# A per-token threshold search by bisection: 16 steps instead of 18, and the interval held as lower end and half width

## The reference

```python
xn = _layernorm(x)                          # x: (2, 4096, 4096)

s = silu(einsum('bsh,ih->bsi', xn, w_gate)) # I = 11008 values per token
k = int(0.5 * I)
_, idx = top_k(-abs(s), k)                  # the k smallest in magnitude ...
s[rows, idx] = 0.0                          # ... are set to zero, token by token
s = s * einsum('bsh,ih->bsi', xn, w_up)
attn = einsum('bsi,hi->bsh', s, w_down)

base = einsum('bsd,od->bso', xn, W_base) + b_base
gate = softmax(xn @ W_gate.T)               # 8 experts of rank 16
thr = sigmoid(xn @ W_thr + b_thr) * 0.125
w = max(gate - thr, 0), normalized
moe = einsum('ner,ne,eor->no', xn @ A_w, w, B_w) * 2
out = x + attn + base + moe
```

## Time and profile before

| | us |
|---|---|
| the two timed runs | 5919.37, 6205.86 |
| their median | 6062.61 |
| the profiled execution | 5898.11 |
| its span, slowest core (core 2) | 5896.6 |
| spans of all eight cores | 5871.0 to 5896.6 |
| TensorE busy | 4396.2 (75% of the span) |
| VectorE busy | 1320.0 (22%) |
| ScalarE busy | 1240.5 (21%) |

### The profile page before, as it was taken

How to read it: one execution, slowest core, us unless ns; L and a number is a source line. 1 busy time by engine, 2 the same in 40 slices (tenths; PEclk the granted TensorE clock), 3 DMA queues, 4 the chain that set the end, 5 groups by cost and what they waited for, 6 DMA issues and landing times.

```text
span 5896.6 us, 51357 instructions; the slowest of 8 cores (5871.0 to 5896.6 us)
## 1 busy us (share of the span) xinstructions
PE 4396.2 (75%) x20408; PEld 1983.5 (34%) x20408; DVE 1320.0 (22%) x1928; ACT 1240.5 (21%) x1522; POOL 546.6 (9%) x640
## 2 busy tenths in 40 slices
PE   5999957600399977999859998675004999788988
PEld 2444523200144443433324444232002444333333
DVE  2000052688510000000020000536884001000000
ACT  2000043566400022000020001436663000320000
POOL 0111101000011100111101111010000111001110
PEclk9999978855699977999969999787557999779999
DMA  6999967700399955999959999576004999569999
GB/s 119 146 147 146 126 91 108 112 0 0 49 151 150 151 85 77 171 167 167 165 115 147 145 148 129 82 123 96 0 0 62 150 150 150 72 92 162 168 169 146
DMA packets 669369, 683.02 MB, mean 116 GB/s; under 512 B 31184, under 2 KB 651728, under 8 KB 668112
## 3 DMA queue, kind: packets, MB, share of 16 engines
q0 software_dynamic: 631120, 612.61, 74.0%
q1 hardware_dynamic: 38016, 67.13, 3.7%
HBM read 1267.07 MB, written 25.17 MB: 219 GB/s over the span
## 4 chain that ended last, share of the span: by engine, by line
PE 65%; ACT 12%; DMA 11%; DVE 6%; issue 5%; DVEq 0%; ACTq 0%; SPq 0%; POOLq 0%; POOL 0%
PE q L370 20%; PE q L476 19%; PE q L519 16%; ACT sc L604 10%; PE q L428 8%; DMA wst<-wdT 6%; DMA wst<-wbT 3%; PE pt L492 2%; ACT S L627 1%; DVE st L769 1%; DMA ovr<-x 1%; DVE lns L665 1%; DVE S L828 0%; ACT S L553 0%; ACT sc L627 0%
## 5 line engine op out<-in xcount | busy, mean ns | idle before, releaser
L476 PE MATMUL q<-wst,xT 128*128 128x512 f16 (+1 forms) x5632 | 1203.6, 375 | 870.5 <-DVE S L828 850.6
L370 PE MATMUL q<-wst,xT 128*128 128x512 f16 (+1 forms) x5632 | 1219.3, 375 | 25.3 <-ACT S L553 9.4
L519 PE MATMUL q<-wst,S 128*128 128x512 f16 x4128 | 1145.3, 386 | 17.1 <-DVE ovr L847 16.8
L476 PEld LDWEIGHTS q<-wst,xT 128*128 128x128 f16 x5632 | 549.1, 98 | 1525.4 <-issue 905.6
L604 ACT ACTIVATE sc<-ovr,st 128x6400 f16<-128x6400 f16 x144 | 810.6, 5629 | 254.5 <-DVE st L806 214.9
L370 PEld LDWEIGHTS q<-wst,xT 128*128 128x128 f16 x5632 | 548.2, 98 | 696.1 <-issue 84.9
L781 DVE TENSOR_SCALAR_CACHE_REDUCE sc<-ovr,st 128x4608 f16<-128x4608 f16 x144 | 721.8, 5012 | 65.5 <-ACT sc L604 47.9
L519 PE MATMUL q<-wst,sc 128*128 128x512 f16 x1376 | 531.7, 386 | 85.0 <-DMA wst<-wdT 84.6
L519 PEld LDWEIGHTS q<-wst,S 128*128 128x128 f16 x4128 | 409.5, 99 | 522.9 <-issue 56.9
L428 PE MATMUL q<-wst,xT 128*128 128x512 f16 x2048 | 475.3, 397 | 145.7 <-DMA wst<-wbT 145.7
L842 DVE TENSOR_TENSOR ovr<-q,ffst 128x512 f32<-128x512 f32 x64 | 44.2, 690 | 1526.1 <-PE q L519 1321.4
(11 more groups left out here) (79 smaller groups left out, 1094.1 us busy)
## 6 DMA issues: line engine op xcount, KB each, us to landing
wst<-wgT POOLq DMA_DIRECT2D x168, 1024.0 KB, 9.6
wst<-wuT POOLq DMA_DIRECT2D x168, 1024.0 KB, 11.2
wst<-wdT POOLq DMA_DIRECT2D x160, 1024.0 KB, 11.7
wst<-wbT POOLq DMA_DIRECT2D x64, 1024.0 KB, 11.2
ovr<-x SPq DMA_DIRECT2D x8, 2048.0 KB, 8.7
xs<-x SPq DMA_DIRECT2D x64, 256.0 KB, 10.4
y<-ovr SPq DMA_DIRECT2D x64, 256.0 KB, 7.9
wst<-wdT POOLq DMA_DIRECT2D x16, 768.0 KB, 9.7
```

What stands on the lines that cost most here:

```text
L370: mm = mark(tensor.matmul(quad[m][:, 0:wl], xT[:, k * 512 + m * 128: k * 512 + (m + 1) * 128], wst[:, slot * SLOTB + kk * wl: slot * SLOTB ...
L476: mm = mark(tensor.matmul(bk[:, 0:wl], xT[:, k * 512 + m * 128: k * 512 + (m + 1) * 128], wst[:, slot * SLOTB + kk * wl: slot * SLOTB + (k ...
L519: mm = mark(tensor.matmul(bk[:, 0:512], lhs, wst[:, slot * SLOTB + kk * 512: slot * SLOTB + (kk + 1) * 512], start=(k == 0), stop=(k == IT ...
```

## The change

The number of iterations goes from 18 to 16. The interval is no longer kept by its two ends but by `lo` and `wdh`, half its width; `wdh` takes the column of `hi`. The maximum goes to `mid` first, is halved into `wdh` and copied to `mid`. In each iteration the count is turned into a 0 or 1 in fp32 (`predf`, which is `cu`), one instruction adds `predf * wdh` to `lo`, one halves `wdh`, and one adds `lo` and `wdh` to the new `mid`. After the last iteration VectorE waits for its own last `mid`, doubles `wdh` again and adds it to `lo`, which gives the upper end in the place of `mid`; the masks take that as `hi`. The interval ends four times as wide. ScalarE's program changes in the number of passes alone; TensorE's, GpSimd's and SyncE's don't change.

```diff
--- before.py
+++ after.py
@@ -23,7 +23,7 @@
 NW = len(WINS)
 NWV = O // 512
 SUB = 8
-ITERS = 18
+ITERS = 16
 SEL_L = 4608
 SEL_R = I - SEL_L
 K_TOP = I // 2
@@ -762,18 +762,19 @@
                             di(ins)
                 for m in range(NT):
                     lo = st[:, 3 * m:3 * m + 1]
-                    hi = st[:, 3 * m + 1:3 * m + 2]
+                    wdh = st[:, 3 * m + 1:3 * m + 2]
                     mid = st[:, 3 * m + 2:3 * m + 3]
+                    predf = cu[:, :]
                     vector.wait_ge(aGE, n_aGE(c, NW - 1, m))
                     n = di(vector.memset(lo, 0.0))
-                    n = di(vector.reduce_max(hi, S[:, m * I:(m + 1) * I],
+                    n = di(vector.reduce_max(mid, S[:, m * I:(m + 1) * I],
                                              axis=mybir.AxisListType.X,
                                              apply_absolute_value=True))
                     dw(n)
-                    n = di(vector.tensor_add(mid, lo, hi))
-                    dw(n)
-                    dc(vector.tensor_scalar(out=mid, in0=mid, scalar1=0.5,
-                                             scalar2=None, op0=OP.mult), vMID)
+                    n = di(vector.tensor_scalar(out=wdh, in0=mid, scalar1=0.5,
+                                                scalar2=None, op0=OP.mult))
+                    dw(n)
+                    dc(vector.tensor_copy(mid, wdh), vMID)
                     for it in range(ITERS):
                         vector.wait_ge(vMID, n_vMID(c, m, it))
                         if it == 0:
@@ -788,24 +789,29 @@
                         vector.wait_ge(aCR, n_aCR(c, m, it))
                         dw(n)
                         n = di(vector.scalar_tensor_tensor(
-                            out=cu[:, :], in0=cl[:, 1:2], scalar=0.5,
+                            out=predf, in0=cl[:, 1:2], scalar=0.5,
                             in1=cl[:, 0:1], op0=OP.mult, op1=OP.add))
                         dw(n)
                         n = di(vector.tensor_scalar(
-                            out=pred[:, 0:1], in0=cu[:, :], scalar1=K_EFF,
-                            scalar2=None, op0=OP.is_ge))
-                        n = di(vector.tensor_scalar(
-                            out=pred[:, 1:2], in0=cu[:, :], scalar1=K_EFF,
+                            out=predf, in0=predf, scalar1=K_EFF,
                             scalar2=None, op0=OP.is_lt))
                         dw(n)
-                        n = di(vector.copy_predicated(hi, pred[:, 0:1], mid))
-                        n = di(vector.copy_predicated(lo, pred[:, 1:2], mid))
+                        n = di(vector.scalar_tensor_tensor(
+                            out=lo, in0=predf, scalar=wdh, in1=lo,
+                            op0=OP.mult, op1=OP.add))
+                        n = di(vector.tensor_scalar(
+                            out=wdh, in0=wdh, scalar1=0.5, scalar2=None,
+                            op0=OP.mult))
                         dw(n)
-                        n = di(vector.tensor_add(mid, lo, hi))
-                        dw(n)
-                        dc(vector.tensor_scalar(
-                            out=mid, in0=mid, scalar1=0.5, scalar2=None,
-                            op0=OP.mult), vMID)
+                        dc(vector.tensor_add(mid, lo, wdh), vMID)
+                    vector.wait_ge(vMID, n_vMID(c, m, ITERS))
+                    n = di(vector.tensor_scalar(
+                        out=wdh, in0=wdh, scalar1=2.0, scalar2=None,
+                        op0=OP.mult))
+                    dw(n)
+                    n = di(vector.tensor_add(mid, lo, wdh))
+                    dw(n)
+                    hi = mid
                     n = di(vector.tensor_scalar(
                         out=junkL, in0=sab[:, 0:SEL_L], scalar1=hi,
                         scalar2=None, op0=OP.is_gt))
```

## The result

| | before | after |
|---|---|---|
| profiled execution | 5898.11 us | 5771.03 us |
| its span, slowest core | 5896.6 | 5769.1 |
| median of the cores' spans, cores 0-3 / 4-7 | 5878.8 / 5877.2 | 5740.4 / 5740.6 |
| timed runs, lowest | 5910.79 | 5761.71 |
| timed runs, median of all | 6064.0 (10 runs) | 5961.85 (11 runs) |

The kernel is 2.46% faster. In 7 of the 11 runs of after the cores of one die were granted a lower TensorE clock than the others (in the run of 5990.26 us 0.83 to 0.84 against 0.88) and took 3 to 9% longer, 5 of the 10 runs of before are longer too, by 5 to 9%, and the ratio is that of the other runs, whose medians are 5772.4 and 5918.2 us, 145.8 apart.

The account below looks back on a forecast made before the run. Mostly TensorE and weights bound the span, with the search exposed before the up projection; per chunk 59.5 + 14.8 - 1.1 + 0.4 = 73.6, two chunks 147 us off 5898.1, giving 5751 us; range 5730 to 5785, reported time 5725 to 5910.

Parts of the forecast that it names:

- 286 / 2 = 143 us higher, at 5894: Upper reach of the reported time if it is a median over runs 286 us apart; with scatter 5910.
- the chances named for over 2%: Chance of being faster by over 2%, given as 0.88, beside 0.09 for within 2% and 0.03 for slower.
- Eight passes a chunk, 59.5 us: Exposed search stretch before the up projection: 44 passes left instead of 52, 8 x 7.44 = 59.5 us gained per chunk.
- rival 3: Exposed search: only passes of m = 1 to 3 count, 6 fewer exposed, 118 us gained, 5780 us; chance 0.04.
- The tail, 1.19 for 1.55 us: VectorE's small instructions ending each iteration: 0.36 us less, period 7.08 us, 41 x 0.36 = 14.8 us gained per chunk.
- Rivals 1 and 2: Iteration tail: the first, no shrinking, 5781 us; the second, shrinking by instruction count, 0.44 saved, 5742 us; chance 0.06 each.
- The group end, 0.37 us more: VectorE from `cu` to first mask: 1.74 us against 1.37, three times exposed, 1.1 us lost per chunk.
- Ahead of the base stage, 0.4 us: First base-stage matmul stands behind transposes freed after passes 1 and 2; one shorter tail counts, 0.4 us gained.
- The switch stays hidden, cost 0: Token-group switch moves one wave earlier, to wave 6, still covered by its matmuls with 5.9 us to spare; cost 0.
- The stall, 348 us: TensorE's wait before L476, up projection: shrinks from about 421 by 73 to 348 us, still released by L828.
- Rival 4: Up projection after the stall: TensorE longer at low clock, 2% slower from 1,200 more slow matmuls on; chance 0.03.
- Rival 5: End of the stall: weights, not the search, release L476, so the gain is hidden; 5898 us; chance 0.03.

Follow-up runs that it names:

- Packed passes: Changed kernel, 16 iterations, ScalarE's 16 pairs of copies moved behind other passes, so 34 passes run under the base stage instead of 20; ratio to before 0.9303.

## Why the prediction was right or wrong

**Where it was wrong.** The reported time, 5961.85 us, lies 52 us over the range's end of 5910. The step that failed is the last one of the range, "286 / 2 = 143 us higher, at 5894". It took half the distance of two unequal runs for the worst that a median can do. That holds for a median of two, and even there it was counted from the lower run: the median of the two lay 164.5 us over the profiled execution (6062.61 and 5898.11). Of the eleven runs of after seven took 5940.89 us or more, so the median is simply one of those, here 191 us over the profiled 5771. From the two runs that I had, the end should have been the forecast plus the full 286 us at the least, 6037, or the range should have been stated for executions like the profiled one alone (5730 to 5785 held both the profiled 5771 and the 5772 of such runs). It was a wrong step about what a median over mixed runs is, not about the kernel. Two sums are also a little off: 5894 and 20 of scatter make 5914, and the chances named for over 2% add up to 0.89.

**The base.** The sum stood on 5898.1 us, and the runs of before that compare with it have a median of 5918.2. So 5751 came out 21 us low, with the difference of 147 us against 145.8 measured. The ratio's interval reaches from 136 to 155 us, so that they come so close is in part luck. The profiled executions differ by 127 us, as the slowest core of after lies 29 us over the median of the cores and that of before 19; the medians of the cores differ by 137.

**Where the 137 us come from.** I compare the stages, each from its first matmul to the first of the next, as means of the eight cores and for the two chunks. The up projection up to the end of the stall is shorter by 72.8 and 75.7 us (450.0 to 377.2, and 451.2 to 375.5). The base stage keeps its length within 1 us (333.5 and 334.2, 330.2 and 329.3), and so does the up projection behind the stall (577.9 in both, 577.8 and 578.5). The down projection is 3 and 6 us longer (694.3 to 697.4, 674.7 to 680.7). There is one trace of before. In the traces of the eleven experiments the two down projections take 1373 to 1386 us together, 1369 in that of before and 1378 in that of after. Whether these 9 us belong to the change or to the one execution is not shown.

**Eight passes a chunk, 59.5 us:** right, 60.4 with that half of the change alone. That passes dropped from m = 0 count in full (the step against rival 3) is shown by the kernel that dropped those alone.

**The tail, 1.19 for 1.55 us:** right, 1.18. The form that had no row, a `scalar_tensor_tensor` with its scalar from memory, took 0.22 us, and its follower came 0.14 after it (1307.45 to 1307.59), for the 0.13 taken from the copy pair. Rivals 1 and 2, periods of 7.44 and 7.00, fell with the 7.08.

**The group end, 0.37 us more:** 1.72 for 1.74 us behind `cu`, and 1.38 before, so 0.34.

**Ahead of the base stage, 0.4 us:** right. The last transpose of `h16` waits 0.37 us less for its copy, in before and in after:

```profile
778.22 0.26 PE L414 MATMUL pt<-eye,h 128*128 128x128 f16 x1 [12.27 <-ACT hwT L577]
...
774.23 0.26 PE L414 MATMUL pt<-eye,h 128*128 128x128 f16 x1 [11.90 <-ACT hwT L577]
```

**The switch stays hidden, cost 0:** right. ScalarE idles 6.46 us behind it, for 5.9 expected. The kernel with 15 iterations shows that this hung on the even count: put between two pairs of copies, the switch cost TensorE 4.4 to 6.8 us a chunk, by core.

**The stall, 348 us:** right, 346.75 and 345.72.

**Rival 4 (low clock after the stall)** didn't occur. In the first 4 us of the up projection's return TensorE ran 12 matmuls at a granted clock of 0.63, against 8 at 0.50 before, and from there the stretch is as long as before (577.9 us, as above):

```profile
1495.00:1499.00 4.00, 3.84 (x12) 1.38 (x13) 1.80 (x4) 0.00 (x0) 0.00 (x0) 0.63 0.58 182
```

Rival 5 (no change) didn't either: L476 is still released by the search.

## What to carry to other kernels

When a stretch has one engine pair computing and the rest waiting, count what lies behind the last point at which other work is tied to it. Work dropped ahead of that point counts as much as work behind it if the interleave goes by position. In a loop of one long pass and a short tail, shorten the chain that depends on the operand that lands last, and prepare everything else while waiting; the number of instructions is not the measure. And before dropping iterations, look how much of the search could run in the idle time that is already there: that was worth more here, on top of the change, than the change itself (253.7 us of TensorE's waits for the search against 148.7; by the ratios 267 and 146).

## What the runs showed that I had not expected

The sum over small instructions held to a few hundredths of a microsecond each: 0.25 to 0.27 us from one to the next that waits for it (0.31 where the one ahead is a copy of 0.21 us), 0.07 where nothing is waited for, 0.13 to 0.14 behind one with a [128,1] scalar from memory, and 0.32 from the start of such an instruction to ScalarE's next pass (1302.81 to 1303.13), for 0.25 behind one without (1307.84 to 1308.09).

Packed passes did not slow the matmuls or the weights beside them: 42.6 us a wave with up to five passes in it, 42.4 with two. Over the eight cores the base stage takes 334.2 and 330.4 us in the two chunks, 334.2 and 329.3 in after.

The first iteration of a group is longer than the others in every kernel: 12.15 us in after, where the others take 7.08. In it VectorE's count begins only when ScalarE's pass has ended, which the program asks for with a wait (`aCR` for `it == 0`). Two of these lie in each of after's stalls. What an earlier start would give was not tried.
